# Start-up of a five-stage transformer-block pipeline: weight loads, masks, buffer clears and set-up waits moved between engines

## What is computed

```python
x = x + tanh(g_xattn[0]) * performer(layernorm(x), ctx, ctx, features)      # causal linear attention, 16 heads
x = x + tanh(g_ffn[0])   * rwkv_ffn(layernorm(x), W_r, W_k, W_v, mu_r, mu_k)
x = x + tanh(g_xattn[1]) * gated_attention(ctx, layernorm(x), w_kv, w_q, w_la, w_proj, b_proj, att_w)
x = x + tanh(g_ffn[1])   * bitnet_ffn(layernorm(x), w_gate, w_up, w_down)    # ternary weights, 8-bit activations
```

## Time and profile before

| | us |
|---|---|
| median of 3 runs | 525.05 |
| lowest and highest | 523.63, 532.01 |
| the profiled execution | 527.92 |
| its span in the profile | 526.2 |

### The profile page before, as it was taken

How to read it: one execution, slowest core, us unless ns; L and a number is a source line. 1 busy time by engine, 2 the same in 40 slices (tenths; PEclk the granted TensorE clock), 3 DMA queues, 4 the chain that set the end, 5 groups by cost and what they waited for, 6 DMA issues and landing times.

```text
span 526.2 us, 18953 instructions
## 1 busy us (share of the span) xinstructions
PE 448.9 (85%) x7552; PEld 333.5 (63%) x7586; DVE 419.6 (80%) x1372; ACT 371.7 (71%) x769; POOL 301.3 (57%) x416
## 2 busy tenths in 40 slices
PE   3578889899999999999999999999999999766832
PEld 1245658686767676767767676767676867554621
DVE  6453576798989898989898989899898988888534
ACT  1353575778787878788787978797878787766423
POOL 8022248484848575666666666657575848473510
PEclk9587999999999999999999999999999999999555
DMA  6401010101001020101010101010101000000000
GB/s 203 119 2 38 7 39 15 32 4 37 19 20 35 2 51 4 51 4 49 4 48 8 47 9 44 11 44 11 43 12 42 13 14 12 11 11 12 2 10 10
DMA packets 31526, 15.15 MB, mean 29 GB/s; under 512 B 12496, under 2 KB 30800, under 8 KB 31440
## 3 DMA queue, kind: packets, MB, share of 16 engines
q1 hardware_dynamic: 30144, 13.58, 9.7%
q10 hardware_dynamic: 1296, 0.36, 0.3%
HBM read 9.73 MB, written 2.10 MB: 22 GB/s over the span
## 4 chain that ended last, share of the span: by engine, by line
PE 62%; ACT 13%; POOL 9%; DVE 7%; issue 5%; DMA 2%; ACTq 1%; POOLq 0%; DVEq 0%
PE TP L1480 11%; PE MC L1513 9%; PE FP L1388 7%; PE MA L1404 6%; PE FP L1367 4%; POOL ft L394 4%; ACT ft L605 3%; ACT ft L606 3%; PE FP L1371 3%; PE FP L1369 3%; PE SP L1471 3%; ACT E L642 3%; PE SP L1584 2%; DVE WT L969 2%; PE FP L1330 2%
## 5 line engine op out<-in xcount | busy, mean ns | idle before, releaser
L394 POOL TENSOR_SCALAR ft<-ft 128x512 f32<-128x512 f32 x64 | 39.5, 617 | 79.6 <-ACT ft L606 57.4
L1513 PEld LDWEIGHTS MC<-Vc,ET 128*64 128x64 f32 x2048 | 67.7, 142 | 27.1 <-issue 26.7
L1513 PE MATMUL MC<-Vc,ET 128*64 128x25 f32 x2048 | 74.0, 221 | 2.7 <-ACT ET L647 2.3
L417 POOL TENSOR_TENSOR Zn<-E,rsh 128x1024 f32<-128x1024 f32 x32 | 60.9, 1902 | 11.6 <-DVE rsh L1029 11.4
L425 POOL TENSOR_TENSOR Zn<-Zn,Gs 128x1024 f32<-128x1024 f32 x32 | 60.9, 1902 | 3.2 <-DVE Gs L1040 1.7
L653 ACT ACTIVATE ET<-TP 128x512 f32<-128x512 f32 x64 | 38.0, 596 | 28.0 <-PE TP L1480 28.0
L1388 PE MATMUL FP<-ft 32*64 32x64 f32 x2048 | 38.0, 222 | 14.9 <-POOL ft L394 11.4
L969 DVE TENSOR_TENSOR WT<-FP,mask 128x512 f32<-128x512 f32 x64 | 43.5, 680 | 8.7 <-PE FP L1388 8.6
L1388 PEld LDWEIGHTS FP<-ft 32*64 32x64 f32 x2048 | 34.4, 135 | 23.1 <-issue 19.0
L1009 DVE TENSOR_REDUCE mx<-SP 128x16 f32<-128x1024 f32 x32 | 39.0, 1219 | 6.6 <-PE SP L1471 6.5
L647 ACT ACTIVATE ET<-TP 128x512 f32<-128x512 f32 x64 | 38.0, 596 | 7.2 <-PE TP L1480 6.3
(11 more groups left out here) (200 smaller groups left out, 1171.4 us busy)
## 6 DMA issues: line engine op xcount, KB each, us to landing
Cd<-in_ctx SPq DMA_DIRECT2D x32, 128.0 KB, 2.9
kX<-kT SPq DMA_DIRECT2D x256, 8.0 KB
X<-in_x SPq DMA_DIRECT2D x16, 128.0 KB, 2.3
call<-in_ctx SPq DMA_DIRECT2D x4, 512.0 KB, 9.8
out_x<-X SPq DMA_DIRECT2D x16, 128.0 KB, 1.9
wffn<-in_L_ffn_w_gate SPq DMA_DIRECT2D x1, 256.0 KB, 5.9
wffn<-in_L_ffn_w_up SPq DMA_DIRECT2D x1, 256.0 KB, 6.2
wffn<-in_L_ffn_w_down SPq DMA_DIRECT2D x1, 256.0 KB, 7.1
```

The source lines that it names most:

```text
L394: pool.tensor_scalar(f, f, EPS_K, 1.0, ALU.add, ALU.mult).then_inc(s("ftp"), 1)
L417: pool.tensor_tensor(z, E1[u][:, :].rearrange("p (h m) -> p h m", m=64), rsh[u][:, :].unsqueeze(2).to_broadcast([P, H, 64]), ALU.subtract) ...
L1513: last = mm(MC[64 * j:64 * j + 64, c + 32 * q:c + 32 * q + 25], weights[:, q, 64 * j:64 * j + 64], Vc[g.p][:, 2 * u + j, q, 0:25], start=T ...
```

## The change

ACT's DMA list shrinks to six. `rrep` goes first, `wkv` and `wla` get a semaphore `wv_in`, for which `split_values` waits (32). `wqn`, `wpr` and `bpr` are issued by SP, between `mus` and `wffn`. ACT's Tanh moves ahead of step 0, and ACT writes the four blocks of `gmask`. `Nh` and `Rf` count on a new semaphore `feat` (5), on which PE's `constants` waits; `setup` is now 11. DVE makes `Wqs` and `bpr` at the end of `weights0_turned`. On POOL the two clears of `kX` move to step 1, ahead of `add_X1`; the wait for `setup` moves to step 2, ahead of `with_bias`. ACT's `round_weights` waits for `setup` too. PE warms 9 times at the start behind `cst` 6; the other counts go from 8 to 0 (`rows_T`), 0 to 2 (ahead of `features(a, 0)`), 12 to 14 and 4 to 3 (`prepare`), 4 to 0 (`weights_turn`) and 2 to 1 (`ffn0_out`).

```diff
@@ sync
+            sp.dma_start(wqn[:, :], w_q).then_inc(s("w1_in"), 16)
+            sp.dma_start(wpr[:, :], w_proj).then_inc(s("w1_in"), 16)
+            sp.dma_start(bpr[:, :], b_proj.partition_broadcast(P)).then_inc(s("w1_in"), 16)
             sp.dma_start(wffn[:, 0, :]...
@@ gpsimd
-            pool.tensor_scalar(Nh[:, :, :], blk[:, :, :], -0.5 * S2, 1.0, ALU.mult, ALU.mult).then_inc(s("setup"), 1)
+            pool.tensor_scalar(Nh[:, :, :], blk[:, :, :], -0.5 * S2, 1.0, ALU.mult, ALU.mult).then_inc(s("feat"), 1)
...
                 if b:
+                    if b.first:
+                        clear_keys()
                     add_X1(b)
...
                 if c:
+                    if c.first:
+                        wait_setup()
                     with_bias(c)
...
                     if a.first:
-                        prepare()
+                        clear_values()
                     ftp(a, 0)
@@ scalar
+            act.dma_start(rrep[:, :], feats.unsqueeze(0).to_broadcast([H, DH, MF])).then_inc(s("r_in"), 16)
...
-            act.dma_start(rrep[:, :], feats.unsqueeze(0).to_broadcast([H, DH, MF])).then_inc(s("r_in"), 16)
-            act.dma_start(wkv[:, :], w_kv).then_inc(s("w1_in"), 16)
-            act.dma_start(wla[:, 0:H], w_la).then_inc(s("w1_in"), 16)
-            act.dma_start(wqn[:, :], w_q).then_inc(s("w1_in"), 16)
-            act.dma_start(wpr[:, :], w_proj).then_inc(s("w1_in"), 16)
-            act.dma_start(bpr[:, :], b_proj.partition_broadcast(P)).then_inc(s("w1_in"), 16)
+            act.dma_start(wkv[:, :], w_kv).then_inc(s("wv_in"), 16)
+            act.dma_start(wla[:, 0:H], w_la).then_inc(s("wv_in"), 16)
+            act.wait_ge(s("g_in"), 48)
+            act.activation(tg[:, :], gains[:, 0:4], ACT.Tanh).then_inc(s("tg"), 1)
             act.wait_ge(s("cst"), CST)
+            act.wait_ge(s("cstv"), 1)
+            for b in range(4):
+                r = slice(32 * b, 32 * b + H)
+                act.activation(gmask[r, H * (b // 2):H * (b // 2) + H], ident[r, 32 * b:32 * b + H], ACT.Copy, scale=0.5)\
+                    .then_inc(s("setup"), 1)
+            act.wait_ge(s("tg"), 1)
...
-                act.wait_ge(s("w1_in"), 80)
+                act.wait_ge(s("wv_in"), 32)
...
             def round_weights():
 
+                act.wait_ge(s("setup"), SETUP)
@@ vector
-                v.wait_ge(s("w1_in"), 80)
-                v.tensor_scalar(Wqs[:, :], wqn[:, :], float(DH) ** -0.5, None, ALU.mult).then_inc(s("setup"), 1)
-                v.tensor_scalar(bpr[:, :], bpr[:, :], tg[:, 1:2], None, ALU.mult).then_inc(s("setup"), 1)
...
                 v.tensor_scalar(WvT[:, :], TP[:, 2 * P:3 * P], hB[:, 0:1], None, ALU.mult).then_inc(s("setup"), 1)
+                v.wait_ge(s("w1_in"), 48)
+                v.tensor_scalar(Wqs[:, :], wqn[:, :], float(DH) ** -0.5, None, ALU.mult).then_inc(s("setup"), 1)
+                v.tensor_scalar(bpr[:, :], bpr[:, :], tg[:, 1:2], None, ALU.mult).then_inc(s("setup"), 1)
@@ tensor
             pe.wait_ge(s("wz"), 1)
+            pe.wait_ge(s("cst"), 6)
+            warm(9)
+            pe.wait_ge(s("cst"), CST)
```

More of the change, by code:

```diff
@@ L225, in build @@
         CST = 13
-        CSTV = 4
-        EARLY = 9
-        SETUP = 16
+        CSTV = 5
+        SETUP = 11
         STEPS = NG + STAGES - 1
@@ L322, in _, with clear_keys, clear_values @@
                 pool.wait_ge(s("cst"), 12 + h)
-            pool.tensor_scalar(Nh[:, :, :], blk[:, :, :], -0.5 * S2, 1.0, ALU.mult, ALU.mult).then_inc(s("setup"), 1)
-            def prepare():
+            pool.tensor_scalar(Nh[:, :, :], blk[:, :, :], -0.5 * S2, 1.0, ALU.mult, ALU.mult).then_inc(s("feat"), 1)
+            def clear_keys():
                 for i in range(2):
                     pool.memset(kX[i][:, :, :, :], 0.0).then_inc(s("kX_zero"), 1)
+            def clear_values():
                 for i in range(2):
@@ L338, in prepare, with wait_setup @@
                         pool.wait_ge(s("Vc_one"), n)
+            def wait_setup():
                 pool.wait_ge(s("setup"), SETUP)
@@ L511, in prepare @@
             def prepare():
-                act.wait_ge(s("g_in"), 48)
-                act.activation(tg[:, :], gains[:, 0:4], ACT.Tanh).then_inc(s("tg"), 1)
                 for c in range(4):
@@ L518, in prepare @@
                     act.activation(csq_all[:, c % 2, :], call[:, 8 * c:8 * c + 8, :], ACT.Square).then_inc(s("csq_all"), 1)
-                act.wait_ge(s("tg"), 1)
                 act.wait_ge(s("nkst"), 1)
             def round_weights():
+                act.wait_ge(s("setup"), SETUP)
                 act.wait_ge(s("wrec"), 1)
@@ L783, in link @@
                 v.wait_ge(s("dve_setup"), chain[0])
+            v.memset(gmask[:, :], 0.0).then_inc(s("cstv"), 1)
             v.memset(wz[:, :], 0.0).then_inc(s("wz"), 1)
-            link(v.memset(gmask[:, :], 0.0))
             for t in yP:
@@ L795, in constants @@
                 v.wait_ge(s("cst"), CST)
[L796 to L799, removed]
                 v.wait_ge(s("r_in"), 16)
@@ L804, in constants @@
                                            rrep[:, :].unsqueeze(1).to_broadcast([P, 4, MF]), ALU.mult, ALU.mult)\
-                        .then_inc(s("setup"), 1)
+                        .then_inc(s("feat"), 1)
             def prepare():
@@ L1266, in _ @@
             mm = pe.matmul
-            pe.wait_ge(s("wz"), 1)
-            pe.wait_ge(s("cst"), CST)
             def warm(n):
@@ L1274, in warm @@
                     mm(TP[:, 512:1024], identb[:, :], wz[:, :], start=True, stop=True)
+            pe.wait_ge(s("wz"), 1)
+            pe.wait_ge(s("cst"), 6)
+            warm(9)
+            pe.wait_ge(s("cst"), CST)
             def constants():
-                pe.wait_ge(s("setup"), EARLY)
+                pe.wait_ge(s("feat"), 5)
             def prepare():
-                warm(12)
+                warm(14)
                 pe.wait_ge(s("cmin"), 1)
@@ L1287, in prepare @@
                 mm(SP_[:, 0:1], onesm[0:1, :], cmin1[:, :], start=True, stop=True).then_inc(s("cminB"), 1)
-                warm(4)
+                warm(3)
             def weights_total():
@@ L1628, in step @@
                     if c.first:
-                        warm(2)
+                        warm(1)
                     ffn0_out(c)
@@ L1658, in step @@
                 if a:
-                    if a.first:
-                        warm(8)
                     rows_T(a)
@@ L1683, in step @@
                         constants()
+                        warm(2)
                     features(a, 0)
```

## The result

Four runs of the changed kernel gave a median of 520.85 us (520.15 to 521.64); the kernel before stood at 526.15 beside them. The ratio is 0.990 with a 95% interval of 0.986 to 0.994: faster by 1%, which is less than the 2% of the verdict. A later set gave 521.29 against 527.42, ratio 0.989 (0.985 to 0.992), so the gain is 5 to 6 us. The profiled execution took 520.15 us, its span is 518.4.

A forecast was written before the change was run, and what follows sets the result against it. Start-up waits over the first 60 us were taken as the bound, later steps untouched. 2.5 (`prepare`) + 1.6 (POOL) + 0.5 (clock) + 0.7 (`weights_turn`) + 0.2 (`ffn0_out`) = 5.5, from 525.05 to 519.5 us; range 515.5 to 523.0.

The forecast's parts named there:

- Own semaphore: ACT's start-up wait: value weights land at 14.2 us, so ACT starts 2.95 us sooner and `cmin` is ready at 21.8.
- The reading of 12.1: `wla`'s DMA row gives 12.1 us; taken as when the shared semaphore had counted 32, true landing between 12.1 and 17.1.
- What else could be late on ACT: Gains wait, Tanh and mask blocks ahead of `yA`: `y_A` ends at 12.5, cost nothing, 1.1 us to spare.
- Dummies in `prepare`: Fourteen PE dummies end at 23.9, so the `cmin` transpose moves from 26.4: gain 2.5 us, between 1.8 and 3.4.
- POOL's wait: `ft` additions before `weights0` no longer wait for `setup`: gain 1.6 us, plus 0.5 (0 to 0.8) from step 1's clock.
- No dummies in `weights_turn`: `rows_BT` starts 1.3 us sooner, but half clock may slow features and `weights0`: between +1.3 and -0.7, taken 0.7.
- One dummy fewer in `ffn0_out`: One PE dummy matmul fewer in `ffn0_out`: gain 0.2 us.
- Clears in step 1: POOL's `kX` clears may hold DVE's `wtb` and delay `X1` and `nb_B` by 1.6 us, covered: cost 0, at most 0.3.
- C: Rival, 0.13: gains or weights come 2 to 3 us later than taken, the front gains nearly nothing: 522.4 us.
- D: Rival, 0.05: PE stays at 1.2 GHz from 15 us through step 2 (70 us): 529.5 us.
- B: Rival, 0.06: full clock from the ninth dummy on, `cmin` becomes the bound, gain 10.6: 514.4 us.
- A: Rival, 0.15: weights land at 12.1 and the clock behaves, gain 8.3: 516.8 us.

The follow-up runs named there:

- the old dummies: Changed kernel with all dummy matmul counts and places of the kernel before: 519.38 us, ratio to before 0.985, against 521.29 for the changed kernel.
- squares first with the fill: Changed kernel, old dummies but 6 in `prepare`, ACT squaring two context chunks before the value-weights wait, 5 dummies before step 1's features: 516.59 us, ratio 0.977 to 0.984.
- sets 1 and 3: Groups of runs sharing a chip with runs of the kernel before, whose median was 527.42 us in set 1 and 527.70 in set 3.
- six dummies fewer: Changed kernel with old dummies and two context chunks squared before the value-weights wait, `prepare` dummies cut from 12 to 6: 519.15 us, against 519.12 with twelve.

## Why the prediction was right, point by point

The time (519.5 forecast, 520.85 measured), the range (515.5 to 523.0) and the verdict held. The waits that were to shrink were the right ones, and two of them carry the whole gain. That the number came so close is in part luck. In the pair of profiles the spans differ by 7.8 us, not by 5.5. What was taken as 2.5 + 1.6 + 0.5 came out at 3.8 + 1.6 + 2.0, with small rests the lead of 7.6; then 0.9 was lost where 0.9 (0.7 + 0.2) was to be gained, and the tail gave 1.1. The medians differ by 5.3: the profile of the changed kernel is of its fastest execution, that of the kernel before is above its median.

- *Own semaphore.* 14.2 taken, 13.4 to 14.2 in the eight profiles in which ACT waits for these weights alone; the first at 13.56. The reading of 12.1 as a count and not as a landing was right.
- *What else could be late on ACT.* `y_A` was to end at 12.5 and ended at 12.16. The gains landed later than taken (10.2, not 9.35), but the table load ran ahead of the wait, at 4.51. Right, by the cancelling of two small errors; of the 1.1 us to spare 0.4 were there.
- *Dummies in `prepare`.* Gain 2.5 taken, 3.8 measured in the profile: 0.5 from the earlier weights, 0.8 because the clock rose earlier in the block (14 in 4.41 us, where I took 5.2). That is beyond the end of the range (3.4). How long the block takes differs from run to run: 4.1 and 5.7 us for the same fourteen in two other profiles. By the pace of 0.41 the slow end is 24.5 and not 24.6.
- *POOL's wait.* Direct gain 1.6, forecast and measured. Its effect through the clock was put at 0 to 0.8 in step 1's `weights0` and taken as 0.5; the 0.8 came, and the features of step 1 (1.2 us) with it in this profile, which the sum didn't have. Behind the own semaphore it is worth about 5 us, the largest single part; I had it second. Moved alone it brings 3.0 by the ratio, no more than the semaphore's 2.7 within the noise.
- *No dummies in `weights_turn`: the step that failed.* I took +0.7 between +1.3 and -0.7. The runs give about -1.5 (two profiles) to -1.7 (medians of two sets; -1.9 on one chip for all the old dummies). The saving was 1.2, as put. But the half clock took 0.4 on `rows_BT` itself, 1.3 on the features, 0.4 on the dummies and `ffn0_in` ahead of `weights0`, where PE and no longer POOL ends the wait, and 0.6 on `weights0`: 2.7 in all, of which I had listed 1.9 and counted a third. One dummy fewer in `ffn0_out` gave its 0.2 (from the end of the first part of `weights0` to the second 1.96 instead of 2.18).
- *Clears in step 1.* Cost 0 taken. `wtb` was held for 2.2 us instead of 1.6, and with it `X1`, which I had listed as a sign of being wrong; `nb_B` still came in time, with 0.2 us left and not 3, so "cost 0" was close to failing. Of the 5.72 us of `gmask` 4.9 were waiting, not 5.1: the first operation lasted 5.10, one alone takes 0.17. The Trainium skill (SBUF — State Buffer, "Who interferes with whom") has the other engine wait out a whole instruction; the trace shows more than that, since `wtb` started at 34.60 under the first of two clears (1.81 us each) and was held through both (POOL ended at 36.99).
- *Rivals.* C's late gains came (10.2) and cost nothing. D, the clock, was the right thing to fear, but took back some 2.7 us and not 10. B's sum takes `cmin` at 20.8, where my own forecast had it at 21.8; with that it is 9.6 and not 10.6, 515.4. A and B did not come in the changed kernel; that of squares first with the fill reaches A's time (516.6 against 516.8) by an edit of its own.

The earlier start did reach the end: 6.7 us at 60 us and at 433, 7.8 us in the span. The last 1.1 us came in the tail, where the last three slices of the clock row read 7, 6, 5 instead of 5, 5, 5; the step that I took for a plain carry-over is one only up to there. These are two single executions; over the medians of the two sets the gain is 5.3 and 6.1.

Left open: the masks on ACT, the three DMAs on SP's queue and the late clears were only taken away together, on a kernel with the old dummies; that one of them gains what another loses is not excluded, and parts under about 1.5 us would not show in these intervals. Open is also what sets the moment at which the clock rises or falls.

## What to carry to other kernels

A wait on a shared semaphore counted to its last DMA, and one wait for "all of the set-up" on an engine that needs little of it, were two small edits worth 7.8 us of 527 (6.3 to 9.4); look for these before moving work between engines. Price an idle stretch of TensorE by what runs behind it, at both clock levels: shortening one brought about 5 us for 1.6 of direct work, and taking dummies out of another lost some 1.7 us though nobody reads their result. A lead gained early can be lost at a later stage that falls to half clock: six dummies fewer gained 2.5 us in the profile, and all of it was given back until five were put where PE idled.

## What the runs showed that was not expected

- A small DMA can be among the slowest: the third gain, 0.5 KB, took 7.4 us from issue to landing in the changed kernel while `rrep`, 16 KB but first on the same queue, took 2.3.
- Four VectorE operations of 16 by 16 elements took 5.72 us beside four GpSimd clears (7.30 to 12.62): the first lasted 5.10 us and ended behind the last clear, not between two.
- The spread of the runs is part of the result. The kernel before went from 524.0 to 531.8 us in 23 runs, the changed one from 520.6 to 523.2 in six. At the ends of the spread the time goes with the mean granted clock: in sets 1 and 3 the executions of the kernel before with 0.964 or 0.965 took 523.3 to 524.7 us, those with 0.930 took 531.5 to 532.0. The profiles of one start-up differ in where the clock stands at half; that this makes the spread is inferred, not shown.
